# Eleven more filler matmuls in a decoder layer on one core, and a new order of every engine's units

## What is computed

```python
def attn(x, query_proj, key_proj, value_proj, output_proj):
    q = jnp.einsum('bnd,hkd->bnhk', x, query_proj)      # key dim 16
    k = jnp.einsum('bnd,hkd->bnhk', x, key_proj)
    v = jnp.einsum('bnd,hvd->bnhv', x, value_proj)      # value dim 64
    sim = jnp.einsum('bnkh,bmhk->bnhm', q, k)
    attn = jax.nn.softmax(sim * 0.25, axis=1)
    o = jnp.einsum('bnhm,bmhv->bnhv', attn, v)
    return jnp.einsum('bnhv,dhv->bnd', o, output_proj)
...
x = x + attn(layernorm(x), ...)
x = x + xattn(ctx, ctx, layernorm(x), fm_w, fm_b, fc_w, fc_b)   # exp feature maps, 64 context rows
x = x + ffn(layernorm(x), W_r, W_k, W_v, mu_r, mu_k)            # sigmoid(r) * (relu(k)**2 @ W_v), token shift
```

## Time and profile before

| | |
|---|---|
| median of 3 runs | 462.02 us (461.20 to 463.01) |
| the profiled execution, device time | 463.88 us |
| its span, first to last instruction | 462.1 us |
| PE busy, DVE busy, ACT busy, POOL busy | 435.8, 374.8, 299.3, 135.7 us |
| mean granted clock of TensorE | 0.972 of full speed |
| chain that ended last, by engine | PE 78%, DVE 8%, ACT 4%, issue 3%, DMA 3% |

### The profile page before, as it was taken

One profiled execution on the slowest core, in us unless ns is written; L12 is line 12 of the kernel. 1 busy time (PEld: TensorE's weight loads), 2 busy tenths in 40 slices (PEclk: granted clock), 3 DMA queues, 4 the chain that ended last, 5 costly groups with the idle time before them and its releaser, 6 DMA issues.

```text
span 462.1 us, 8164 instructions
## 1 busy us (share of the span) xinstructions
PE 435.8 (94%) x2716; PEld 273.7 (59%) x2716; DVE 374.8 (81%) x689; ACT 299.3 (65%) x732; POOL 135.7 (29%) x181
## 2 busy tenths in 40 slices
...
PEclk9797999999999999999999999999999999999699
...
GB/s 284 184 222 246 153 47 0 48 136 138 223 53 48 0 1 48 115 182 32 197 0 2 159 3 45 160 137 90 140 1 24 94 1 1 0 42 5 2 1 45
DMA packets 22561, 38.23 MB, mean 83 GB/s; under 512 B 2808, under 2 KB 7160, under 8 KB 22392
## 3 DMA queue, kind: packets, MB, share of 16 engines
q1 hardware_dynamic: 22520, 37.71, 24.3%
...
...
## 4 chain that ended last, share of the span: by engine, by line
PE 78%; DVE 8%; ACT 4%; issue 3%; DMA 3%; SPq 2%; POOL 1%; ACTq 0%; DVEq 0%; POOLq 0%
PE av_bank L720 21%; PE m_bank L652 10%; PE s_pair L706 7%; PE m_bank L656 7%; PE m_bank L868 3%; PE m_bank L772 3%; PE m_bank L856 3%; ACT e_sb L959 3%; PE m_bank L793 2%; PE m_bank L928 2%; DVE nmax L1158 2%; PE m_bank L737 2%; PE m_bank L917 2%; PE m_bank L939 2%; PE m_bank L756 1%
## 5 line engine op out<-in xcount | busy, mean ns | idle before, releaser
L959 ACT ACTIVATE e_sb<-s_pair,nmax 128x512 f32<-128x512 f32 x256 | 173.4, 690 | 49.5 <-DVE nmax L1158 49.2
L1158 DVE TENSOR_REDUCE nmax<-s_pair 128x2 f32<-128x1024 f32 x128 | 152.6, 1212 | 12.7 <-PE s_pair L706 12.3
L720 PE MATMUL av_bank<-e_sb,v_sb 128*64 128x512 f32 x512 | 125.1, 609 | 3.1 <-POOL v_sb L1430 2.8
L1430 POOL TENSOR_TENSOR v_sb<-v_sb,rsum 128x256 f32<-128x256 f32 x64 | 39.7, 621 | 210.2 <-DVE rsum L1166 188.8
L720 PEld LDWEIGHTS av_bank<-e_sb,v_sb 128*64 128x64 f32 x512 | 31.4, 137 | 57.5 <-issue 49.3
L706 PE MATMUL s_pair<-q_st,k_st 64*128 64x512 f32 x256 | 49.7, 453 | 4.6 <-ACT e_sb L959 4.4
L959 ACT ACTIVATION_READ_ACCUMULATOR e_sb<-s_pair,nmax 128x1 f32 x256 | 52.9, 206 | 0.0
L706 PEld LDWEIGHTS s_pair<-q_st,k_st 64*128 64x128 f32 x256 | 20.8, 185 | 52.7 <-issue 27.6
L1457 POOL TENSOR_TENSOR sx<-sx,xrec 128x512 f32<-128x512 f32 x24 | 24.9, 1044 | 41.0 <-DVE xrec L1339 41.0
L652 PE MATMUL m_bank<-wo_hi,ot_hi 128*128 128x256 f32 x128 | 36.6, 292 | 0.0
L656 PE MATMUL m_bank<-wo_lo,ot_hi 128*128 128x256 f32 x128 | 35.0, 279 | 0.0
(11 more groups left out here) (176 smaller groups left out, 813.0 us busy)
## 6 DMA issues: line engine op xcount, KB each, us to landing
...
```

The source lines that it names most:

```text
L720: mm = pe.matmul(av_bank[n % AV_BANKS][64 * par:64 * par + 64, :], v_sb[:, m, 2 * p + par, :], e_sb[:, (4 * q + 2 * i + par) % E_RING, :], ...
L959: act.activation(e_sb[:, g % E_RING, :], s_pair[k // 2][:, k % 2, :], ACT.Exp, bias=nmax[:, g % 8:g % 8 + 1], accum_out=esum[:, q % 4, k:k ...
L1158: dve.tensor_reduce(nmax[:, at:at + 2], s_pair[i][:, :, :], AX_X, ALU.max, negate=True)\
L1430: pool.tensor_tensor(v_sb[:, m:m + 2, 2 * p:2 * p + 2, :], v_sb[:, m:m + 2, 2 * p:2 * p + 2, :], rsum[:, q % 4, :].rearrange("p (m h) -> p ...
```

## The change

Eleven filler units are added on PE: tags -1, -2 and -3 with one matmul each (operands of zeros) at the start, and tags 9 to 16 with one each in the tail. The others get new slots. Ahead of t1(0) stand now warm 0 (two matmuls), -1, -3, -2 and 2 (two): seven matmuls; warm 1 (two) stands between t1(1) and the first qk. In the tail the order is: warm 8 and 13 ahead of z(0); 6, 12 and 10 between t2(1) and xs(0); 11, 7, 9, 14, 4 and 5 between xs(0) and xs(1); 15 behind xs(3); 3 behind pt(3,1); 16 behind pv(1).

All other units stay, with new slots in all five tables, and so a new order in places. At the start, PE goes qk(0,0), first(0), qk(0,1), first(1), v(0,2), qk(1,0), scores(0), where it went qk(0,0), qk(0,1), first(0), first(1), qk(1,0), v(0,2), scores(0). ACT evacuates t1(0) ahead of cutting wqk, and cuts both halves of wv before it evacuates qk(0,1); POOL does its part of the second half ahead of the first scale. SP goes o, x1, feat, qk(0,0), fc, qk(0,1), ld(1), ld(2), qk(1,0), rest, ld(3), where it went o, qk(0,0), qk(0,1), fc, x1, ld(1), ld(2), feat, qk(1,0), qk(1,1), ld(3), ld(4), ld(5), rest. In the tail, fk(1) of batch 2 goes ahead of the last weigh on PE and its mix ahead of the last rsum on DVE, op(1,0) and op(1,1) follow the last weigh as before, fr(1) goes ahead of t2(0); z(1) goes behind xs(1), pt(0,0) ahead of xs(3); on DVE, op(1,1) goes ahead of the normalisation of ln2(0), and fv(1) of batch 2 stands directly ahead of xs(0,0); on ACT, t2(1) goes ahead of z(0,1). No instruction of any other unit is changed.

The diff, cut to the start and the tail (in PLAN, and in the lines left out, only slots change):

```diff
 LAST = [
-    ("op", (1, 0), dict(pe=40, dve=39)),
...
-    ("op", (1, 1), dict(pe=70, dve=70)),
...
-    ("t2", (1,), dict(pe=707, act=184, dve=194)),
-    ("z", (0,), dict(pe=448)),
-    ("z", (0, 1), dict(act=158)),
-    ("xs", (0, 0), dict(dve=207, act=202)),
...
-    ("xs", (0,), dict(pe=1693)),
...
-    ("xs", (1,), dict(pe=1724)),
...
-    ("z", (1,), dict(pe=1708)),
...
-    ("pt", (0, 0), dict(pe=2332, act=956)),
-    ("pt", (0, 1), dict(pe=2332, act=1355)),
...
-    ("xs", (3,), dict(pe=2281)),
...
-    ("pv", (1,), dict(pe=3252)),
...
-    ("fk", (1,), dict(pe=4775, act=4562, dve=4559)),
...
-    ("fv", (0,), dict(pe=4602, dve=4538, sp=4597)),
...
+    ("op", (1, 0), dict(pe=32, dve=41)),
...
+    ("op", (1, 1), dict(pe=34, dve=50)),
...
+    ("t2", (1,), dict(pe=660, act=121, dve=167)),
+    ("z", (0,), dict(pe=561)),
+    ("z", (0, 1), dict(act=125)),
+    ("xs", (0, 0), dict(dve=572, act=130)),
...
+    ("xs", (0,), dict(pe=1062)),
...
+    ("xs", (1,), dict(pe=2084)),
...
+    ("z", (1,), dict(pe=2091)),
...
+    ("pt", (0, 0), dict(pe=2310, act=923)),
+    ("pt", (0, 1), dict(pe=2318, act=1234)),
...
+    ("xs", (3,), dict(pe=2310)),
...
+    ("pv", (1,), dict(pe=3462)),
...
+    ("fk", (1,), dict(pe=5314, act=5173, dve=5163)),
...
+    ("fv", (0,), dict(pe=5234, dve=5243, sp=5244)),
...
 DEFER = [
-    ("mix", (1,), dict(dve=19)),
-    ("fr", (1,), dict(pe=101, act=100)),
-    ("fk", (1,), dict(pe=88, act=94, pool=18)),
-    ("fv", (1,), dict(pe=169, dve=170, sp=167)),
...
+    ("mix", (1,), dict(dve=-3)),
+    ("fr", (1,), dict(pe=77, act=77)),
+    ("fk", (1,), dict(pe=25, act=25, pool=14)),
+    ("fv", (1,), dict(pe=214, dve=197, sp=212)),
...
 FIRST = [
-    ("warm", (0, 2), dict(pe=-521)),
-    ("warm", (1, 2), dict(pe=-455)),
-    ("warm", (2, 2), dict(pe=-2489)),
-    ("ln1", (0,), dict(dve=-2718, pool=-2445, do=-2442)),
-    ("ln1", (1,), dict(dve=-2447, pool=-2435, do=-2442)),
-    ("cut", ("first",), dict(act=-1290, dve=-1301)),
-    ("cut", ("qk",), dict(act=-2394, dve=-2442)),
-    ("t1", (0,), dict(dve=-2405, pe=-38, act=-2372)),
-    ("t1", (1,), dict(pe=-35, act=-2325, dve=-2390)),
-    ("first", (0,), dict(pe=-29, act=-55, dve=-49)),
-    ("first", (1,), dict(pe=-18, act=-33, dve=0)),
-    ("qk", (0, 0), dict(dve=-448, sp=-676, pe=-35, act=-447)),
-    ("qk", (0, 1), dict(pe=-35, act=-141, dve=-119, sp=-484)),
-    ("cut", ("v0",), dict(act=-61, dve=-7)),
-    ("cut", ("v1",), dict(act=22, pool=25)),
-    ("ld", (1,), dict(sp=-145)),
-    ("load", ("o",), dict(sp=-2085)),
-    ("ld", (2,), dict(sp=-136)),
-    ("load", ("x1",), dict(sp=-373)),
-    ("load", ("fc",), dict(sp=-452)),
-    ("load", ("rest",), dict(sp=142)),
-    ("load", ("feat",), dict(sp=-89)),
-    ("v", (0, 0), dict(pe=24, act=22)),
-    ("v", (0, 1), dict(pe=22, dve=24)),
-    ("v", (0, 2), dict(pe=-2, act=9)),
-    ("v", (0, 3), dict(pe=37, dve=30)),
+    ("warm", (0, 2), dict(pe=-2864)),
+    ("warm", (1, 2), dict(pe=-59)),
+    ("warm", (2, 2), dict(pe=-393)),
+    ("ln1", (0,), dict(dve=-2796, pool=-2776, do=-2729)),
+    ("ln1", (1,), dict(dve=-2730, pool=-2768, do=-2729)),
+    ("cut", ("first",), dict(act=-990, dve=-983)),
+    ("cut", ("qk",), dict(act=-2613, dve=-2650)),
+    ("t1", (0,), dict(dve=-2679, pe=-109, act=-2674)),
+    ("t1", (1,), dict(pe=-74, act=-1076, dve=-2625)),
+    ("first", (0,), dict(pe=-40, act=-67, dve=-40)),
+    ("first", (1,), dict(pe=-11, act=-25, dve=-24)),
+    ("qk", (0, 0), dict(dve=-629, sp=-628, pe=-52, act=-626)),
+    ("qk", (0, 1), dict(pe=-26, act=-142, dve=-303, sp=-302)),
+    ("cut", ("v0",), dict(act=-595, dve=-574)),
+    ("cut", ("v1",), dict(act=-242, pool=-37)),
+    ("ld", (1,), dict(sp=-301)),
+    ("load", ("o",), dict(sp=-2065)),
+    ("ld", (2,), dict(sp=-290)),
+    ("load", ("x1",), dict(sp=-679)),
+    ("load", ("fc",), dict(sp=-305)),
+    ("load", ("rest",), dict(sp=47)),
+    ("load", ("feat",), dict(sp=-634)),
+    ("v", (0, 0), dict(pe=25, act=26)),
+    ("v", (0, 1), dict(pe=17, dve=14)),
+    ("v", (0, 2), dict(pe=-11, act=-10)),
+    ("v", (0, 3), dict(pe=39, dve=39)),
...
 ONCE = [
-    ("cut", ("o",), dict(act=3, pool=33)),
-    ("cut", ("fc",), dict(act=244, pool=247)),
-    ("feat", (), dict(sp=90, dve=87, act=83)),
-    ("kf", (0,), dict(pe=97, act=102)),
-    ("kf", (1,), dict(pe=143, act=169)),
-    ("warm", (3, 1), dict(pe=3236)),
-    ("warm", (4, 1), dict(pe=4144)),
-    ("warm", (5, 1), dict(pe=1621)),
-    ("warm", (6, 1), dict(pe=2929)),
-    ("warm", (7, 1), dict(pe=2667)),
-    ("warm", (8, 1), dict(pe=4467)),
+    ("cut", ("o",), dict(act=6, pool=29)),
+    ("cut", ("fc",), dict(act=251, pool=251)),
+    ("feat", (), dict(sp=105, dve=78, act=79)),
+    ("kf", (0,), dict(pe=117, act=129)),
+    ("kf", (1,), dict(pe=154, act=157)),
+    ("warm", (3, 1), dict(pe=3871)),
+    ("warm", (4, 1), dict(pe=3099)),
+    ("warm", (5, 1), dict(pe=3101)),
+    ("warm", (6, 1), dict(pe=1890)),
+    ("warm", (7, 1), dict(pe=2436)),
+    ("warm", (8, 1), dict(pe=1403)),
+    ("warm", (9, 1), dict(pe=2699)),
+    ("warm", (10, 1), dict(pe=2079)),
+    ("warm", (11, 1), dict(pe=2305)),
+    ("warm", (12, 1), dict(pe=2071)),
+    ("warm", (13, 1), dict(pe=1583)),
+    ("warm", (14, 1), dict(pe=2859)),
+    ("warm", (15, 1), dict(pe=3342)),
+    ("warm", (16, 1), dict(pe=4490)),
+    ("warm", (-1, 1), dict(pe=-1193)),
+    ("warm", (-2, 1), dict(pe=-622)),
+    ("warm", (-3, 1), dict(pe=-777)),
...
-ATTENTION = dict(scores=12, weigh=43, max=(10, 11), exp=(15, 15, 17, 18), rsum=25, scale=12, ot_hi=38, ot_lo=43)
+ATTENTION = dict(scores=11, weigh=42, max=(11, 12), exp=(15, 15, 17, 17), rsum=27, scale=12, ot_hi=38, ot_lo=44)
...

```

More of the change, by code:

```diff
@@ new lines @@
+    ("mix", -1, (0,), dict(dve=216)),
+    ("t3", -1, (0,), dict(pe=210, act=204)),
+    ("ln1", 1, (1,), dict(dve=184, pool=160)),
+    ("t1", 1, (1,), dict(dve=200, pe=201, act=199)),
+    ("ln3", -1, (1,), dict(dve=223, pool=225)),
+    ("ld", 0, (7,), dict(sp=191)),
+    ("fc", -1, (1,), dict(pe=200, dve=189)),
+    ("t3", -1, (1,), dict(pe=260, act=262)),
+    ("op", 0, (0, 0), dict(pe=161, dve=166)),
+    ("fr", -1, (0,), dict(pe=255, act=255)),
+    ("fk", -1, (0,), dict(pe=236, act=239, pool=234)),
```

359 lines of the change are left out of this document (174 added, 185 removed).

## The result

The changed kernel takes 455.65 us (median of 5 runs, 455.50 to 455.99), beside 463.01 us for the kernel before on the same chip (5 runs, 461.20 to 464.05). The ratio is 0.9845, 95% interval 0.982 to 0.987: faster by 7.4 us. The profiled run took 455.84 us with a span of 454.0; before these were 463.88 and 462.1. The forecast was 457.4 (454.0 to 462.5), faster.

A forecast was written before the change was run, and what follows sets the result against it. PE was taken as full in the middle, so the first 45 and last 65 us decide: 463.88 - 6.5 (head) + 0.4 (tail) = 457.8 profiled; as median 457.8 or 455.9, the first likelier: 457.4, range 454.0 to 462.5.

The forecast's parts named there:

- Fillers before t1 and in the gap: Start of PE: a seventh filler before t1 and two before the first qk are hidden by waits, cost 0.
- So I take it that the clock holds: PE before the first qk: with the new fillers the full clock stays, scores(0) at 19.1, 2.9 us earlier.
- SP's queue: Head: x1 and feat before the first store send qk(1,0)'s store at 22.4 to 24.4; ACT's 2.84 us stall goes; cost 0.
- The walk: Head, unit by unit: scores(4) at 36.3 instead of 44.35, 8.0 us earlier; after 1.5 taken off, -6.5.
- rival A: Head: fillers don't hold the clock ahead of the first scores; head gives 5.3 less 1.3, time 459.6; chance 0.16.
- Tail, order: Last batch: three moves (mix first, fv(1) before xs(0,0), fillers before xs(1)) sum to +1.5 us at pt(0,1).
- But t2(0) loses it again: Tail: mix and fk(1) moved ahead gain 0.7 us on PE, lost as ln2_do(0) waits behind op(1,1) on DVE.
- xs(0,0) at 417.3 instead of 416.49, +0.8: Tail: fv2(1) on DVE directly ahead of xs(0,0), and z(0,1) behind t2(1)'s evacuation on ACT, delay it 0.8 us.
- The third: Tail: six fillers between xs(0) and xs(1), 2.6 us, make PE fill xs(1) 0.7 us after DVE is free.
- Tail, clock: pt(0,1) to fc(0): a held clock saves 2.3 us; with the order +1.5 or -0.8, the middle +0.4 taken.
- B: Head: a new wait (moved loads or POOL's 4.53 us cut) replaces ACT's stall; about 461.0; chance 0.13.
- C: Tail, xs(0,0) to xn(0,0): DVE's chain costs +4.7, deciding if the head gives under 2; 464.7; chance 0.13.

The follow-up runs named there:

- a_gap_empty: The changed kernel without the two fillers between t1 and the first qk: 456.56 us, ratio 0.9856 to the kernel before.
- a_head_both: The changed kernel without the two fillers between t1 and the first qk and with SP's old start order: 461.91 us, ratio 0.9982.
- b_fill: The kernel before with two more fillers in the gap between t1 and the first qk, six staying ahead of t1: 461.71 us, ratio 0.9978.
- a_mix_clean: The changed kernel with mix(1) behind the last rsum, fk(1) behind op(1,1) and POOL's square of fk(1) behind ln2(0): 457.36 us, ratio 0.9877.
- a_sp_old: The changed kernel with SP's start units in the order of the kernel before: 460.19 us, ratio 0.994.
- a_head_none: The changed kernel without any filler ahead of the first scores: 457.67 us, ratio 0.9915.

## Why the prediction was right, and where its steps were off

**What bounds the kernel.** Right: the middle moved 0.25 us, and nearly all of the 7.4 us come from the first 45 and the last 65 us.

**Fillers before t1 and in the gap.** Right that they are hidden (the first qk came at 10.92 against 10.64, but at 10.56 to 10.95 in the profiled runs of other kernels with the same nine fillers) and that the clock held in this run; scores(0) at 19.47 against 19.1. The step "So I take it that the clock holds", as the work of the two fillers in the gap, was luck in part: a_gap_empty and a_head_both kept the clock in their profiled runs with the gap empty, and b_fill lost it with the gap filled. Every profiled run with seven fillers ahead of t1 kept it; of the three with six, two lost it. Whether the seventh filler or chance decides is open, since no run changed it alone. The 2.9 us that the prediction gave to holding the clock here are what it is worth where it would have fallen; taking the two fillers out cost 0.9 us in the median.

The prediction set this against the Trainium skill ("TensorE: Matmul & The Clock Gate", "Why this matters for your kernels"). The clock at the lower level behind gaps of 1.97 us (a_mix_clean) and 2.33 us still speaks against that rule's longer gaps; a_gap_empty and b_fill (2.14 and 2.06 us, clock held) show that such a gap need not cost it.

**SP's queue.** Right in mechanism: the first half of the store at 24.19 (predicted 22.4 to 24.4 instead of 29.90), no wait of ACT, and a_sp_old gives 4.5 us back. The move cost nothing that the runs show, as taken.

**The walk.** It said -8.0 for scores(4), the trace says -7.03; the step "I take off 1.5" took off 0.5 too much. (The variant with the clock lost once more doesn't add up by 0.5: 2.84 and 2.97 are 5.8, where the walk to 39.0 gives the 5.3 that rival A then uses.) Up to scores(3) the walk was true within 0.4 us: scores(0), scores(1), weigh(0) and scores(2) came at 19.5, 24.5, 26.9 and 28.8 against 19.1, 24.6, 26.9 and 28.9, and scores(3) ended at 33.9 as worked out. It failed in its last step, "v(1,1), weigh(2) to 36.3": by its own prices 33.9 + 1.4 + 1.9 is 37.2, and weigh(2) did start at 35.45, behind the whole of v(1,1).

**Tail, order.** Two of the three terms failed. In the first, mix ahead of the last rsum cost 0.7 us at the last weigh, where about 1.0 was worked out, and fk(1) left the stretch behind it as foreseen. But the step "But t2(0) loses it again" is wrong. ln2_do(0) did go behind op(1,1) on DVE, and that held xn(0) up by about 0.5 us (rstd was done at 400.6, xn(0) started at 401.13), but fr(1) kept PE busy meanwhile: PE had no idle time from the last weigh to z(0), which came 7.63 us earlier than before (412.80 to 405.17) although two fillers now stand ahead of it. a_mix_clean puts the gain of mix first at 1.1 to 1.7 us, where the sum had none. The second step, "xs(0,0) at 417.3 instead of 416.49, +0.8", did not come: xmax moved by -7.14, a little more than the head. The third was mis-sized: DVE waits 1.17 us for xs(1), not 0.7, since the six fillers take 2.8 us (409.28 to 412.07) and DVE then waits for the whole of xs(1), 1.16 us: 3.9 us from xmax on, against 2.7 of DVE work. From xmax to pt(0,1) the loss is 1.26, near the +1.5 of the sum, but from the wait alone; that the two agree is luck.

**Tail, clock.** "The clock may hold or not: I take the middle" was a coin; it held in this run. pt(0,1) to the end gives 2.2 where 2.3 was worked out.

**Sum.** Head 0.5 too small; tail order 0.35 too dear (from scores(4) to pt(0,1) the loss was 7.03 - 5.88 = 1.15, where +1.5 stood); tail clock 1.1 too careful (2.2 where half of 2.3 was taken). These are the 1.96 us between 457.8 and the 455.84 of the profiled run. The question of the 1.86 us between profiled run and median was answered rightly: of the 54 runs of the kernel before beside the variants, those with a mean granted clock of 0.972 took 463.7 to 464.5 us and those with 0.981 took 461.3 to 462.7, and after the change the profiled run lies 0.19 us above the median.

**Rivals.** A did not happen in the profiled run of the changed kernel; a_head_none, whose first matmuls run at the lower level, shows a loss of 2.0 us at scores(0). B did not: scale(2) came last, as foreseen (34.48, behind POOL's 4.54), and PE did not wait for it. C, the DVE chain, is real (1.26 us) but far from 4.7, and the head gave more than the 2 us from which it decides.
